# One transposing matmul a pair instead of two, with new instruction orders on every engine

## The chip, the cores and the metric

The kernel runs on one core of a Trainium2 chip. The metric is device time in microseconds (us); of several runs the median counts. One execution was also recorded by the hardware profiler, and all rows below are of that execution.

## The reference

64 samples of 128 channels by 1024 positions pass two residual layers. For sample b:

```
z   = x[b] + w_cond[itok_198[b]]^T @ x[b]              # 128x128 matrix chosen by the sample
out = z + z @ W^T + s * (z @ A^T) @ B^T                # W 1024x1024, adapter of rank 16
A, B, s = lora_A[itok_6[b]], lora_B[itok_6[b]], scalings[itok_6[b]]
```

The adapter has 8 alternatives, the matrix 200. Everything is float32.

## The kernel before

The order of the two layers is exchanged: since the first layer mixes channels and the second mixes positions, the kernel first computes c = x (I + W^T) + adapter and then (I + w_cond)^T c. Samples are taken in 32 pairs. W is cut into 4 by 3 blocks (b00 to b32) of 256 by 342. One pair's big product is a fast matrix multiplication with 19 block products, "17", "5", "15", "13" and so on, in place of 24; their left operands are sums of blocks of x (u, u12, u67, u910, u11, u54, u3 and the plain a001, a02, a03, a1, a13), their right operands sums of W's blocks. Partial results go through six PSUM banks with roles alpha, beta, pi02, pi10, pi11, pi12 that change between even and odd pairs (`BANKS`), and are collected in c10_sb, c11_sb, c12_sb and c02_sb.

For precision each float32 operand is split into a rounded part and a rest (x_hi and x_lo, w_hi and w_lo, z_hi and z_lo, c_hi and c_lo): ScalarE rounds (`copy`), VectorE subtracts, and a product is six TensorE matmuls (two chunks of 128 times three combinations).

The adapter rides along: 16 extra columns on some products give xa = x A^T s, 128 by 16 for each of the two samples. VectorE writes xa and its rest into `xa_cols` (`sum_xa1`, `split_xa1`, `rest_xa1` for sample 1 after product 11; `split_xa0`, `rest_xa0` for sample 0 after product 3). A "turn" is a matmul of xa_cols with an identity that transposes it; ScalarE copies the result to `g_sb` (`turned_xa`), and TensorE multiplies it with `b_stack`, the chosen rows of B, in three `lora` matmuls a sample. Sample 1's are "lora 10, 11, 12", sample 0's "lora 00, 01, 02". Before, turn1 (sample 1, into o_ps) stands behind product 8 and turn0 (sample 0, into the alpha bank) between products 6 and 12, and the three lora matmuls of sample 0 stand behind product 17 of the next pair.

The second layer of pair p is computed during pair p+1: `condition` is three matmuls of 512 columns into o_ps; ScalarE copies o_ps to o_sb (`evacuate`), and SyncE's queue stores it.

The orders are written out by hand: each engine has a program of its own, in which an instruction waits for counters (semaphores) of others and holds up all that stands behind it on its engine. Pairs 0 and 1 are special. Pair 0 is a plain ("dense") product with W's blocks as they land; meanwhile GpSimd adds identities to them (`add_identity`, names i10, i11b, i32 and so on) and VectorE forms the right operands (`add`; the wait `made`). Pair 1 multiplies unsplit float32 operands (`whole_product`) while ScalarE (`in_place`) and VectorE (`split_after`) split the 19 right operands. From pair 2 on all is split; pairs 4 to 29 run in a loop. Adapter rows are split once, saved to DRAM (`save_b`, b_split) and gathered from there for each pair (`load_b`, copied by `take_b`).

## Time and profile before

| | |
|---|---|
| median of 3 runs | 771.11 us (771.02 to 771.27) |
| the profiled execution | 771.08 us, of which the recorded span is 769.2 us |
| TensorE matmuls (PE) | 761.3 us busy, 99% of the span, 4432 instructions |
| VectorE (DVE) | 612.7 us, 80% |
| ScalarE (ACT) | 504.3 us, 66% |
| GpSimd (POOL) | 196.8 us, 26% |
| granted TensorE clock | 1.00 in every slice |
| DMA | 128 GB/s on average, 321 GB/s in the first of 40 slices |

The span runs from the first to the last recorded instruction. Busy time of TensorE is the union of overlapping matmuls: each is recorded from its start to the modelled end of its last column, so the distance between two starts, not the recorded length, is what one matmul costs.

### The profile page before, as it was taken

The numbers are of one execution on the slowest core, as the hardware profiler recorded it, in microseconds if no ns is written. First come the engines' busy times: TensorE is split into PE (matmuls) and PEld (weight loads), VectorE is DVE, ScalarE is ACT, GpSimd is POOL, SyncE is SP. The second block draws the span as 40 slices with busy tenths as digits, with TensorE's granted clock in tenths as the row PEclk, the third lists the DMA queues.
The fourth block names the chain that finished last, engine by engine and source line by source line (L and its number), as shares of the span: only waits on it lengthen the run. The fifth ranks groups of instructions, "written<-read, shape, count | busy, mean of one in ns | idle before, by whom it ended". The sixth has DMA issues, their size and how long they took to land.

```text
span 769.2 us, 16746 instructions
## 1 busy us (share of the span) xinstructions
PE 761.3 (99%) x4432; PEld 721.5 (94%) x4432; DVE 612.7 (80%) x1386; ACT 504.3 (66%) x1173; POOL 196.8 (26%) x428
## 2 busy tenths in 40 slices
PE   8999999999999999999999999999999999999998
PEld 5667999999999999999999999999999999999997
DVE  6899977879777788777888777888777888777774
ACT  3476666676666676666676666676666676666673
POOL 5633211332311333212333211333212233212200
PEclk9999999999999999999999999999999999999999
DMA  9333334442334342334442343442343432343222
GB/s 321 138 131 144 124 121 147 125 149 90 111 128 147 125 148 86 116 127 139 134 144 80 114 140 129 143 132 84 124 137 123 150 129 84 121 143 123 89 90 83
DMA packets 47291, 98.32 MB, mean 128 GB/s; under 512 B 6438, under 2 KB 25894, under 8 KB 47270
## 3 DMA queue, kind: packets, MB, share of 16 engines
q1 hardware_dynamic: 46832, 97.68, 37.6%
q10 hardware_dynamic: 438, 0.39, 0.2%
q8 instruction: 9, 0.15, 0.1%
q14 instruction: 12, 0.10, 0.0%
HBM read 63.45 MB, written 34.60 MB: 127 GB/s over the span
## 4 chain that ended last, share of the span: by engine, by line
PE 90%; DVE 2%; issue 0%; ACT 0%; DVEq 0%; ACTq 0%
PE bank L1394 75%; PE o_ps L1455 4%; PE bank L1433 4%; PE o_ps L1454 4%; PE o_ps L1456 4%; DVE c_sb L904 0%; DVE z_lo L901 0%; DVE x_lo L901 0%; PE o_ps L1445 0%; PE bank L1438 0%; DVE x_raw L901 0%; DVE w_lo L901 0%; ACT z_hi L518 0%; DVE bank L904 0%; PE bank L1454 0%
## 5 line engine op out<-in xcount | busy, mean ns | idle before, releaser
L1394 PE MATMUL bank<-w_hi,x_hi 128*128 128x342 f32 (+2 forms) x1200 | 390.4, 325 | 1.1 <-ACT c_sb L518 1.1
L1394 PE MATMUL bank<-w_lo,x_hi 128*128 128x342 f32 (+2 forms) x1200 | 387.1, 323 | 0.0
L1394 PE MATMUL bank<-w_hi,x_lo 128*128 128x342 f32 (+2 forms) x1200 | 386.5, 322 | 0.0
L1394 PEld LDWEIGHTS bank<-w_hi,x_hi 128*128 128x128 f32 x1200 | 225.8, 188 | 9.7 <-ACT c_sb L518 2.2
L1394 PEld LDWEIGHTS bank<-w_lo,x_hi 128*128 128x128 f32 x1200 | 225.6, 188 | 2.8
L1394 PEld LDWEIGHTS bank<-w_hi,x_lo 128*128 128x128 f32 x1200 | 226.1, 188 | 0.0
L901 DVE TENSOR_TENSOR x_lo<-x_raw,x_hi 128x256 fp32r<-128x256 f32 (+1 forms) x270 | 145.0, 545 | 31.3 <-ACT x_hi L518 26.7
L518 ACT ACTIVATE x_hi<-x_raw 128x256 fp32r<-128x256 f32 (+1 forms) x270 | 133.8, 507 | 53.9 <-PE bank L1394 45.7
L303 POOL TENSOR_TENSOR w_lo<-a_ride,w_hi 128x160 fp32r<-128x160 f32 x30 | 15.6, 521 | 503.5 <-ACT w_hi L518 503.5
L518 ACT ACTIVATE c_sb<-bank 128x342 f32<-128x342 f32 x190 | 85.7, 452 | 41.4 <-PE bank L1394 39.0
L518 ACT ACTIVATE z_hi<-c_sb 128x340 fp32r<-128x340 f32 (+1 forms) x128 | 60.3, 490 | 53.0 <-DVE c_sb L904 53.0
L904 DVE TENSOR_TENSOR c_sb<-bank,c_sb 128x342 f32<-128x342 f32 x186 | 91.1, 504 | 3.6 <-PE bank L1433 2.5
L518 ACT ACTIVATE o_sb<-o_ps 128x512 f32<-128x512 f32 x124 | 73.9, 596 | 12.6 <-PE o_ps L1456 12.6
L901 DVE TENSOR_TENSOR x_lo<-t_sb,x_hi 128x512 fp32r<-128x512 f32 x60 | 41.5, 692 | 36.0 <-ACT x_hi L518 35.9
L901 DVE TENSOR_TENSOR z_lo<-c_sb,z_hi 128x340 fp32r<-128x340 f32 (+1 forms) x128 | 69.6, 545 | 0.4 <-ACT z_hi L518 0.2
L901 DVE TENSOR_TENSOR xa_sum<-bank,c_sb 128x16 f32<-128x16 f32 x31 | 5.4, 174 | 63.1 <-PE bank L1394 63.1
L518 ACT ACTIVATE bank<-bank 128x342 f32<-128x342 f32 (+1 forms) x93 | 41.2, 444 | 16.3 <-PE bank L1394 15.8
L1454 PE MATMUL o_ps<-z_hi,c_hi 128*128 128x512 f32 x126 | 50.5, 401 | 0.0
L1455 PE MATMUL o_ps<-z_lo,c_hi 128*128 128x512 f32 x126 | 49.8, 395 | 0.0
L1456 PE MATMUL o_ps<-z_hi,c_lo 128*128 128x512 f32 x126 | 49.5, 392 | 0.0
L279 POOL TENSOR_TENSOR a_ride<-a_now,s_now 128x32 f32<-128x32 f32 x93 | 43.5, 493 | 17.0 <-DMA a_now<-lora_a 10.2
L1433 PE MATMUL bank<-b_stack,g_sb 128*128 128x340 f32 (+1 forms) x192 | 46.4, 324 | 0.4 <-ACT b_stack L518 0.4
(106 smaller groups left out, 888.1 us busy)
## 6 DMA issues: line engine op xcount, KB each, us to landing
x_raw<-xT SPq DMA_DIRECT2D x62, 512.0 KB, 4.2
out<-o_sb SPq DMA_DIRECT2D x62, 512.0 KB, 2.6
b_stack_raw<-b_split SPq DMA_DIRECT2D x128, 128.0 KB, 2.5
c_raw<-cond_w SPq DMA_DIRECT2D x64, 64.0 KB, 1.7
a_now<-lora_a SPq DMA_DIRECT2D x62, 64.0 KB, 3.2
w_lo_raw<-wB SPq DMA_DIRECT2D x7, 342.0 KB, 8.2
w_hi_raw<-wB SPq DMA_DIRECT2D x5, 342.0 KB, 5.8
out<-x_raw SPq DMA_DIRECT2D x4, 256.0 KB, 2.0
```

The lines of the kernel that those rows point to most:

```text
L279: unit.tensor_tensor(to, a_now[:, n, k:k + count, :], s_now[:, n:n + 1].unsqueeze(2).to_broadcast([P, count, 2 * R]), ALU.mult).then_inc(a ...
L303: unit.tensor_tensor(left_rides(w_lo), rides(0, 5), left_rides(w_hi), ALU.subtract).then_inc(ride_ready, 1)
L518: return nc.scalar.activation(to, x, ACT.Copy)
L901: return nc.vector.tensor_tensor(to, x, y, ALU.subtract)
L904: return nc.vector.tensor_tensor(to, x, y, ALU.add)
L1394: last = nc.tensor.matmul(bank[:, lo:hi], x[:, left, c * C:(c + 1) * C], w[:, c, FIRST[o]:FIRST[o] + WIDTH[o]], start=opens and c == 0 and ...
L1433: nc.tensor.matmul(main_of(bank_of(j, d, role), cols.stop - cols.start), g_sb[n][:, :], b_stack[:, cols], start=False, stop=True, skip_gro ...
L1454: nc.tensor.matmul(bank[:, :], c_hi[:, n, :], z_hi[n][:, cols], start=True, stop=False)
L1455: nc.tensor.matmul(bank[:, :], c_hi[:, n, :], z_lo[n][:, cols], start=False, stop=False)
L1456: nc.tensor.matmul(bank[:, :], c_lo[:, n, :], z_hi[n][:, cols], start=False, stop=True)\
```

## The change

1. Every pair but the last has one turn. Both samples' xa lie in one tile `xa_cols` (rows 0 to 47 and 64 to 111 after the transposition), g_sb of each sample keeps zeros in the other's rows, and ScalarE copies 64 rows for each. The one turn stands between products 19 and 6; the last pair keeps a turn of sample 1 by itself.
2. The end of TensorE's pair is rewritten (`end`): products 1 and 3 before the second `condition`, then 19, the turn, 6, and four lora matmuls (11, 10, 12, 00) before product 12. Two lora matmuls are left behind product 17.
3. ScalarE's and VectorE's pair programs are in another order throughout; pairs 1, 2 and 3 have orders of their own.
4. In the first pair GpSimd reads the adapter numbers before it waits for the table of scalings, and adds b11's identity after the rides of b10 and b00.
5. The two stores of the split adapter rows are issued by ScalarE's queue instead of SyncE's; SyncE gathers pair 0's rows before it loads pair 1's A.

```diff
-             "b11": ("lo", "6"), "b32": ("lo", "16"), "b31": ("lo", "12"), "b02": ("lo", "1"), "b10": ("lo", "3"),
+             "b11": ("lo", "6"), "b32": ("hi", "8"), "b31": ("lo", "12"), "b02": ("lo", "1"), "b10": ("lo", "3"),
...
-    POOL_SUMS = ("i21a", "i21b", "i10", "i11a", "i11b", "i00", "i32", "i22")
+    POOL_SUMS = ("i21a", "i21b", "i10", "i00", "i11a", "i11b", "i32", "i22")
...
-        xa_cols = [sb(f"xa_cols{n}", [P, P], f32) for n in range(2)]
+        xa_cols = sb("xa_cols", [P, P], f32)
...
             def load_b(i, j, d):
                 found = adapters(sp, i, j, d)
-                after(sp, lora_done["00"], i, j, d - 1)
+                after(sp, lora_done["02"], i, j, d - 1)
...
-            sp.wait_ge(b_hi_ready, 1)
-            save_b(0, z_hi[0])
             sp.wait_ge(cond_landed, 16)
             load_c(0, 0, 0)
-            sp.wait_ge(b_lo_ready, 1)
-            save_b(1, z_lo[0])
             sp.wait_ge(adapter_landed, 16)
+            sp.wait_ge(b_saved, 32)
+            load_b(0, 0, 0)
             sp.wait_ge(first_scaled, 8)
             load_a(sp, 0, 0, 1)
-            sp.wait_ge(b_saved, 32)
-            load_b(0, 0, 0)
...
+            first = [pool.value_load(adapter_sb[0:1, n:n + 1], min_val=0, max_val=NAD - 1) for n in range(2)]
             pool.wait_ge(s_tab_ready, 1)
-            pick_scalings(0, 0, 0)
+            for n in range(2):
+                nc.gpsimd.tensor_copy(s_now[:, n:n + 1], s_tab[:, bass.ds(first[n], 1)]).then_inc(s_picked, 1)
...
             add_identity("b10", 0, 256, 0, 86)
-            pool.wait_ge(w_landed["b11"], 16)
-            add_identity("b11", 0, 0, 86, 42)
-            add_identity("b11", 1, 42, 0, 128)
             first_rides("b10")
             pool.wait_ge(w_landed["b00"], 16)
             add_identities("b00", 0)
             first_rides("b00")
+            pool.wait_ge(w_landed["b11"], 16)
+            add_identity("b11", 0, 0, 86, 42)
+            add_identity("b11", 1, 42, 0, 128)
...
             def turned_xa(i, j, d, n):
-                after(act, turned[n], i, j, d)
-                if n:
-                    after(act, lora_done["12"], i, j, d - 1)
+                rows = slice(n * P // 2, (n + 1) * P // 2)
+                alone = n and not exists(i, j, 1)
+                if alone:
+                    act.wait_ge(turned_alone, 1)
                 else:
-                    after(act, lora_done["00"], i, j, d - 1)
-                copy(g_sb[n][:, :], o_ps[1][:, 0:P] if n else bank_of(j, d, "alpha")[:, H - P:H]).then_inc(g_ready[n], 1)
+                    after(act, turned, i, j, d)
+                after(act, lora_done["12" if n else "02"], i, j, d - 1)
+                copy(g_sb[n][rows, :], o_ps[1][rows, 0:P] if alone else bank_of(j, d, "alpha")[rows, H - P:H])\
+                    .then_inc(g_ready[n], 1)
...
+            act.wait_ge(b_hi_ready, 1)
+            save_b(0, z_hi[0])
...
+            act.wait_ge(b_lo_ready, 1)
+            save_b(1, z_lo[0])
...
-            copy_c5(0, 1)
-            hi_z02(0, 1, -1)
-            begin_c10(0, 1)
-            evacuate(0, 1, -1, 1, 0)
+            hi_z02(i, j, -1)
             made(act, "9", "f")
             in_place("9")
-            seed_pi11(0, 1)
-            in_place("8")
-            evacuate(0, 1, -1, 1, 1)
+            evacuate(i, j, -1, 1, 0)
+            begin_c10(i, j)
             made(act, "6", "16")
             in_place("16")
...
+            def end(i, j):
+                left("u3", i, j)
+                multiply("16", "pi12", i, j).then_inc(product_done["16"], 1)
+                after(pe, c02_begun, i, j, 0)
+                left("a001", i, j)
+                multiply("1", "alpha", i, j)
+                multiply("3", "alpha", i, j).then_inc(product_done["3"], 1)
+                if exists(i, j, -1):
+                    condition0(i, j, -1, 1)
+                left("a02", i, j)
+                after(pe, c_block["12"], i, j, -1)
+                multiply("19", "pi02", i, j, True).then_inc(product_done["19"], 1)
+                turn(i, j)
+                after(pe, c02_half, i, j, 0)
+                multiply("6", "beta", i, j).then_inc(product_done["6"], 1)
+                after(pe, g_ready[1], i, j, 0)
+                after(pe, b_ready, i, j, 0)
+                lora("11", i, j, 0)
+                lora("10", i, j, 0)
+                lora("12", i, j, 0)
+                after(pe, g_ready[0], i, j, 0)
+                lora("00", i, j, 0)
+                left("a03", i, j)
+                multiply("12", "beta", i, j).then_inc(product_done["12"], 1)
```

What this does to the order on TensorE at the end of an odd pair of the loop: before, from the first `condition` of sample 0 to the end. Turn1 writes o_ps1, turn0 bank2 (alpha), and xa0_ready and g1_ready are the counters of VectorE's and ScalarE's part of the adapter.

```order
L1456 MATMUL o_ps0<-z_hi0,c_lo 128x512
L1445 MATMUL o_ps1<-ident_r,xa_cols1 128x128 [waits o_out11,xa1_ready]
L1394 MATMUL bank5<-w_hi,x_hi 128x342 [waits u3_ready]
...
L1454 MATMUL o_ps1<-z_hi0,c_hi 128x512 [waits z02_ready,g1_ready]
...
L1394 MATMUL bank2<-w_hi,x_hi 128x358 [waits a001_ready,c02_begun]
...
L1433 MATMUL bank0<-b_stack,g_sb1 128x342 [waits b_ready,g1_ready]
L1433 MATMUL bank1<-b_stack,g_sb1 128x342
...
L1394 MATMUL bank4<-w_hi,x_hi 128x342 [waits c12_summed,a02_ready]
...
L1433 MATMUL bank5<-b_stack,g_sb1 128x340
L1394 MATMUL bank3<-w_hi,x_hi 128x342 [waits c02_half]
...
L1438 MATMUL bank2<-ident_r,xa_cols0 128x128 [waits xa0_ready,a03_ready]
```

And now at the same place:

```order
L1525 MATMUL bank2<-w_hi,x_hi 128x358 [waits a001_ready,c02_begun]
...
L1587 MATMUL o_ps1<-z_hi0,c_hi 128x512 [waits z02_ready,o_out11]
...
L1525 MATMUL bank4<-w_hi,x_hi 128x342 [waits c12_summed,a02_ready]
...
L1571 MATMUL bank2<-ident_r,xa_cols 128x128 [waits xa1_ready,xa0_ready]
L1525 MATMUL bank3<-w_hi,x_hi 128x342 [waits c02_half]
...
L1564 MATMUL bank1<-b_stack,g_sb1 128x342 [waits b_ready,g1_ready]
L1564 MATMUL bank0<-b_stack,g_sb1 128x342
L1564 MATMUL bank5<-b_stack,g_sb1 128x340
L1564 MATMUL bank2<-b_stack,g_sb0 128x342 [waits g0_ready]
L1525 MATMUL bank3<-w_hi,x_hi 128x342 [waits a03_ready]
```

The lora matmuls of both samples now come six matmuls (product 6) behind the one turn, where turn1 had three products and a `condition` between it and its first lora.

ScalarE at the end of an odd pair of the loop, now (before, the two copies to g_sb stood eleven and more instructions apart, each behind its own turn):

```order
L516 ACTIVATE w_hi<-a_ride 128x5x2x16 [waits p3_done,a_summed]
L516 ACTIVATE w_hi<-a_ride 128x4x2x16
L516 ACTIVATE x_hi<-x_raw0 128x256 [waits p19_done,x_landed0_0]
L516 ACTIVATE g_sb1<-bank2 64x128 [waits lora12_done,xa_turned]
L516 ACTIVATE c_hi<-c_raw 128x256 [waits o_done01,ci_summed]
L516 ACTIVATE g_sb0<-bank2 64x128 [waits lora02_done,xa_turned]
L516 ACTIVATE x_hi<-x_raw0 128x512 [waits p6_done,x_landed0_0]
L516 ACTIVATE z_hi0<-bank2 128x342 [waits o_done00,lora00_done]
L516 ACTIVATE o_sb<-o_ps1 128x512 [waits o_done01]
```

What moved: the two g copies stand with one instruction (hi_of_c) between them, behind hi_a02, which waits for product 19.

VectorE between pairs 0 and 1, from the first rest of z on. The rows named w_lo_raw are sums of W's blocks; the one that waits for p17_done is the operand of product 9. Before:

```order
L901 TENSOR_TENSOR z_lo1<-c10_sb,z_hi1 128x342 [waits z10_hi_ready]
L901 TENSOR_TENSOR z_lo1<-c11_sb,z_hi1 128x342 [waits z11_hi_ready]
L1164 TENSOR_TENSOR w_lo_raw<-w_lo_raw 128x2x342 [waits p17_done]
L901 TENSOR_TENSOR z_lo1<-c12_sb,z_hi1 128x340 [waits z12_hi_ready]
L901 TENSOR_TENSOR z_lo0<-bank1,z_hi0 128x342 [waits z01_hi_ready]
L901 TENSOR_TENSOR z_lo0<-bank0,z_hi0 128x342 [waits z00_hi_ready]
```

Now:

```order
L1245 TENSOR_TENSOR w_lo_raw<-w_lo_raw,w_hi_raw 128x2x342 [waits pool_summed]
L964 TENSOR_TENSOR z_lo1<-c10_sb,z_hi1 128x342 [waits z10_hi_ready]
L964 TENSOR_TENSOR z_lo1<-c11_sb,z_hi1 128x342 [waits z11_hi_ready]
L1245 TENSOR_TENSOR w_lo_raw<-w_lo_raw 128x2x342 [waits dve_summed,pool_summed]
L964 TENSOR_TENSOR z_lo0<-bank0,z_hi0 128x342 [waits z00_hi_ready]
L1245 TENSOR_TENSOR w_lo_raw<-w_lo_raw,w_hi_raw 128x2x342 [waits dve_summed,dense_done]
L1245 TENSOR_TENSOR w_lo_raw<-w_lo_raw,w_hi_raw 128x2x342 [waits dve_summed]
L964 TENSOR_TENSOR z_lo1<-c12_sb,z_hi1 128x340 [waits z12_hi_ready]
L964 TENSOR_TENSOR z_lo0<-bank1,z_hi0 128x342 [waits z01_hi_ready]
L1245 TENSOR_TENSOR w_lo_raw<-w_lo_raw,w_hi_raw 128x2x342 [waits p17_done]
```

What moved: z12's rest stands behind four sums (16a, 16, 19a, 19) instead of one, and product 9's sum is the last of all.

## Rows read from the trace of the kernel before

**Rows 1.** The page: busy time of TensorE, and its granted clock in 40 slices.
```profile
PE 761.3 (99%) x4432; PEld 721.5 (94%) x4432; DVE 612.7 (80%) x1386; ACT 504.3 (66%) x1173; POOL 196.8 (26%) x428
...
PEclk9999999999999999999999999999999999999999
```

**Rows 2.** TensorE's waits: waited for, us in total, times, longest.
```profile
PE bank L1566 <- POOL w_hi_raw L465: 1.4, 1, 1.4
...
PE bank L1394 <- ACT c_sb L518: 1.1, 1, 1.1
PE bank L1433 <- ACT b_stack L518: 0.4, 1, 0.4
```

**Rows 3.** TensorE's groups: the two turns (busy us, mean ns).
```profile
L1445 PE MATMUL o_ps<-ident_r,xa_cols 128*128 128x128 f32 x32 | 7.5, 234 | 0.0
L1438 PE MATMUL bank<-ident_r,xa_cols 128*128 128x128 f32 x32 | 7.4, 233 | 0.0
```

**Rows 4.** TensorE in order of time (start, length), around turn1 of a pair.
```profile
406.54 0.32 PE L1394 MATMUL bank<-w_hi,x_lo 128*128 128x342 f32 x1
...
407.39 0.22 PE L1445 MATMUL o_ps<-ident_r,xa_cols 128*128 128x128 f32 x1
407.45 0.37 PE L1394 MATMUL bank<-w_hi,x_hi 128*128 128x342 f32 x1
407.66 0.32 PE L1394 MATMUL bank<-w_lo,x_hi 128*128 128x342 f32 x1
407.82 0.32 PE L1394 MATMUL bank<-w_hi,x_lo 128*128 128x342 f32 x1
```

**Rows 5.** ScalarE in order of time, in the same pair.
```profile
406.90 0.46 ACT L518 ACTIVATE c_sb<-bank 128x342 f32<-128x342 f32 x1 [1.20 <-PE bank L1394]
407.65 0.28 ACT L518 ACTIVATE g_sb<-o_ps 128x128 fp32r<-128x128 f32 x1 [0.30 <-PE o_ps L1445]
407.82 0.60 ACT L518 ACTIVATE o_sb<-o_ps 128x512 f32<-128x512 f32 x1
...
409.84 0.41 ACT L518 ACTIVATE c_hi<-c_raw 128x256 fp32r<-128x256 f32 x1
410.15 0.62 ACT L518 ACTIVATE x_hi<-t_sb 128x512 fp32r<-128x512 f32 x1
```

**Rows 6.** VectorE in order of time, pair 0's sums and first rests of z.
```profile
22.66 0.99 DVE L1164 TENSOR_TENSOR w_lo_raw<-w_hi_raw,w_lo_raw 128x684 f32<-128x684 f32 x1 [0.81 <-POOL w_lo_raw L472]
23.58 0.41 DVE L904 TENSOR_TENSOR x_whole<-x_raw 128x256 f32<-128x256 f32 x1
...
33.79 2.65 DVE L1164 TENSOR_TENSOR w_lo_raw<-w_lo_raw,w_hi_raw 128x684 f32<-128x684 f32 x3
36.36 0.93 DVE L901 TENSOR_TENSOR z_lo<-c_sb,z_hi 128x342 fp32r<-128x342 f32 x2
```

**Rows 7.** ScalarE in order of time, pair 1.
```profile
42.29 0.60 ACT L518 ACTIVATE o_sb<-o_ps 128x512 f32<-128x512 f32 x1 [0.23 <-PE o_ps L1456]
42.78 0.77 ACT L518 ACTIVATE w_hi<-w_lo_raw 128x684 fp32r<-128x684 f32 x1
```

**Rows 8.** TensorE in order of time, pair 1: the second condition, product 2.
```profile
42.98 0.65 PE L1454 MATMUL o_ps<-z_hi,c_hi 128*128 128x512 f32 x1
...
43.94 1.36 PE L1410 MATMUL bank<-w_lo_raw,x_whole 128*128 128x358 f32 x4
```

**Rows 9.** DMA: the second load of pair 1's x, issue and time to landing.
```profile
L336 SPq DMA_DIRECT2D x_raw<-xT x1: 1096/1096/1096, 12.2 to 12.2; - x1
...
DMA to landing us min/median/max: 10.0/10.0/10.0
```

**Rows 10.** DMA: all queues together, 14 to 21 us.
```profile
DMA packets 1602, 2.70 MB, mean 386 GB/s; under 512 B 109, under 2 KB 1360, under 8 KB 1602
```

**Rows 11.** TensorE in order of time, product 2 of pair 2.
```profile
72.11 0.43 PE L1394 MATMUL bank<-w_hi,x_hi 128*128 128x358 f32 x1 [1.06 <-ACT c_sb L518]
72.38 0.33 PE L1394 MATMUL bank<-w_lo,x_hi 128*128 128x358 f32 x1
```

More of the change, by code:

```diff
@@ new lines, in step, with last_step @@
+                hi_u11(i, j, 1)
+                hi_rides(i, j, 1)
+                hi_a02(i, j, 1)
+                turned_xa(i, j, 0, 1)
+                hi_of_c(i, j)
+                turned_xa(i, j, 0, 0)
+                hi_a001(i, j, 1)
+                hi_z00(i, j, 0)
+                evacuate(i, j, -1, 0, 1)
+                hi_z11(i, j, 0)
+                hi_z10(i, j, 0)
+            def last_step(i, j):
+                copy_c17(i, j)
+                hi_a03(i, j, 0)
+                hi_z12(i, j, -1)
+                copy_c5(i, j)
+                hi_z01(i, j, -1)
+                begin_c10(i, j)
+                evacuate(i, j, -1, 1, 0)
+                seed_pi11(i, j)
+                hi_z02(i, j, -1)
+                begin_c11(i, j)
+                hi_u54(i, j, 0)
+                evacuate(i, j, -1, 1, 1)
+                seed_pi10(i, j)
+                take_b(i, j)
+                begin_c12(i, j)
+                seed_pi12(i, j)
@@ new lines, in step @@
+                sum_u3(i, j, 1)
+                rest_u(i, j, 1)
+                rest_u12(i, j, 1)
+                rest_a13(i, j, 1)
+                sum_xa1(i, j)
+                split_xa1(i, j)
+                rest_a1(i, j, 1)
+                clear_beta(i, j)
+                sum_v(i, j, 1)
+                rest_xa1(i, j)
+                sum_u67(i, j, 1)
+                half_c02(i, j)
+                sum_u910(i, j, 1)
+                rest_u67(i, j, 1)
+                sum_u11(i, j, 1)
@@ new lines, in _ @@
+            clear_beta(i, j)
+            rest_a13(i, j, 1)
+            sum_xa1(i, j)
+            rest_a1(i, j, 1)
+            split_xa1(i, j)
+            sum_v(i, j, 1)
+            sum_u3(i, j, 1)
+            sum_u67(i, j, 1)
+            half_c02(i, j)
+            rest_xa1(i, j)
+            split_xa0(i, j)
+            sum_u910(i, j, 1)
+            rest_xa0(i, j)
+            add_identity_c(i, j)
+            sum_u11(i, j, 1)
+            half_c12(i, j)
+            rest_u910(i, j, 1)
@@ L1574, in _ @@
             for _ in range(7):
[L1575 removed]
+                nc.tensor.matmul(o_ps[1][:, 0:P], xa_cols[:, :], xa_cols[:, :], start=True, stop=True)
             dense("b12")
@@ L1598, in _ @@
             pe.wait_ge(ident_r_ready, 1)
-            turn1(0, 0)
-            turn0(0, 0)
+            turn(0, 0)
             made(pe, "i32")
             dense("b32")
+            pe.wait_ge(zeros_ready, 3)
             after(pe, g_ready[1], 0, 0, 0)
@@ L1607, in _ @@
             lora("12", 0, 0, 0)
+            after(pe, g_ready[0], 0, 0, 0)
+            lora("00", 0, 0, 0)
             made(pe, "i22")
```

528 lines of the change are left out of this document (294 added, 234 removed).

## The prediction

> **What bounds the kernel now.** I read the page first. TensorE is busy for 99% of the span and its clock is granted in full in every slice [rows 1], so the end can only move if TensorE gets less to do, or if the few places where it stands still change. Next the list of its waits [rows 2]: 1.4 us for GpSimd's identity in b21, 1.1 us for ScalarE's copy of c10_sb in pair 2, 0.4 us for the adapter rows b_stack in pair 0. The first and the last lie in the first 35 us. There is no wait in pairs 3 to 31. So in the steady part a matmul that goes away is worth exactly what it costs, provided that the new orders of ScalarE and VectorE bring nothing late; in the first three pairs the question is who is late.
>
> **What a turn costs.** There are 32 of each kind, recorded at 0.23 us [rows 3], but that is not the price. In order of time turn1 starts at 407.39, the next product at 407.45 and that product's second matmul at 407.66; ordinary neighbours start 0.16 apart [rows 4]. From the turn to the second matmul it is 0.27, so the turn costs 0.27 - 0.16 = 0.11 us: 0.06 of its own and 0.05 since the following weights could not be loaded behind so short a matmul. The Trainium skill, "TensorE: Matmul & The Clock Gate", section "Back-to-back issue gap", gives some 81 ns for a sustained matmul of 128 columns; by it the 31 turns would be worth 2.5 us as an estimate, while the trace has more, and the trace is taken.
>
> All pairs but the last lose one turn: 31 x 0.11 = 3.4 us. The lora matmuls, products and conditions are the same in number and width, so moving them costs TensorE nothing by itself. The three lora matmuls of sample 0 that stood behind product 17 become two there and one in the group of four.
>
> **Is the new turn in time, and what waits for it?** I lay a pair out around the turn's start, T. Latencies are from the trace: from the start of a product's last matmul to the dependent ScalarE copy 0.36 (406.54 to 406.90); from a turn's start to the copy of g 0.26 (407.39 to 407.65); that copy lasts 0.28 and lets the next start after 0.17; a 256-column copy such as hi_of_c holds ScalarE for 0.31 (409.84 to 410.15) [rows 4, 5]. Product 19's last matmul starts at T-0.16, so hi_a02 starts at T+0.20, the copy of g1 at T+0.51 (end T+0.79), hi_of_c at T+0.68, the copy of g0 at T+0.99 (end T+1.27). TensorE does product 6 in 0.06 + 0.21 + 5 x 0.16 = 1.07 and wants lora 11 at T+1.07, whose weights g1 it wants one matmul earlier, at T+0.91; lora 00 comes three matmuls later, with g0 wanted at T+1.39. Both copies are in time, each by 0.12 us. That is the thinnest margin of the change. On the other side of the turn, xa of sample 0 needs product 3, then VectorE: between product 3 and the turn now lie the second condition and product 19, about 1.6 us, against two small VectorE operations and one 512-column rest between them; an estimate of 0.4 us is left. The other waits that moved (evacuation of o_ps1 now at the very end of a pair, sample 0's z00 rounded before the pair ends, SyncE's store and load of c behind that evacuation) have half a microsecond or more before their reader. I cost them at nothing; they are covered by product 12 and the next pair's product 17.
>
> **The first pair.** GpSimd's earlier read and the later b11 take away most of the 1.4 us, and the rows of B, saved by ScalarE's queue, come before the lora matmuls: up to 1.4 + 0.4 = 1.8 us of lead for TensorE at the start of pair 1 [rows 2]. I do not think that it keeps it. VectorE works without a pause from 23.58 on, through the three sums that end at 36.4, to the rests of z [rows 6]; it is the engine that the start of pair 1 depends on, and what it still has to do grows. Behind those three sums the new order has sum 16a, z10, z11, sum 16, z00, sums 19a and 19, z12, z01, and sum 9. A sum costs 2.65 / 3 = 0.87, a rest of z 0.43 (a pair of them in 0.93, and the next starts sooner) [rows 6]. z12 is thus ready at 36.4 + 4 x 0.87 + 4 x 0.43 = 41.6, sum 9 at 36.4 + 5 x 0.87 + 5 x 0.43 = 42.9. The second condition of pair 1, which stood at 42.98 [rows 8], would want z12 at about 41.2 with the full lead; a first small wait. Then ScalarE: it now does in_place("9"), which waits for the last of VectorE's sums, then the evacuation, and only then begin_c10, for which product 2 waits. The rounding of a whole block holds it for some 0.66, the evacuation for 0.49 (42.29 to 42.78), the copy lasts 0.46 [rows 5, 7]: product 2 cannot start before 42.9 + 0.66 + 0.49 + 0.46 + 0.1 = 44.6. It stood at 43.94 [rows 8].
>
> To this comes a delay D of VectorE's whole row of sums. Below, D is 0, or rather a little less than nothing if the sums find their blocks sooner. Above: VectorE began on pair 1's x at 23.58, the second half of which had landed at 12.2 + 10.0 = 22.2 [rows 6, 9]; the two stores of 0.5 MB each used to stand behind these loads in SyncE's queue and now go beside them. At 386 GB/s over all queues [rows 10] 1 MB is 2.7 us, so x lands up to 24.9 and D is at most 1.3. The Trainium skill says in "DMA: Bandwidth & Descriptors", section "Queues, rings and completion order", that each DMA engine takes turns between the rings of its queues; by that rule the loads would indeed give way to the stores, which speaks for the upper half. No run here shows two such queues side by side yet. I take D = 0.6, between the ends, since the stores need not overlap with all the loads: VectorE has also to wait for GpSimd's b32, once 0.81 us [rows 6], which is now later by b11. Product 2 starts at 45.2, which is 1.3 later than before, with the front's lead gone.
>
> **Pair 2.** Here TensorE stood 1.06 us and restarted at half pace (72.11 to 72.38, 0.27 for 0.16), 1.2 us together [rows 2, 11], because hi_u54, which waited for VectorE, stood ahead of begin_c10 on ScalarE. The new order has begin_c10 ahead of it, and VectorE has left rests out of pair 1's tail. I count the 1.2 us as won.
>
> **The sum.** -3.4 (turns) + 1.3 (product 2 in pair 1) - 1.2 (pair 2) = -3.3; a few tenths more come from having fewer short groups of lora matmuls among the float32 products of pair 1, which I put at 0.2. The profiled execution took 771.08, the median is 771.11, so it is the same base: 771.1 - 3.5 = **767.6 us**.
>
> **The rivals.**
> - *The front's lead is kept.* Sums and z12 come in time (VectorE is faster than its rows, or D is negative), product 2 is not held, and the 1.8 us of waits are won as well. 771.1 - 3.4 - 1.8 - 1.2 - 0.2 = 764.5. For it: all three named waits are dealt with by the change. Against: the ScalarE and VectorE rows as added up above. Chance 0.22.
> - *The loads give way fully, and pair 2 stays late.* D = 1.3 adds 0.7, and VectorE's seven or so splits in pair 2 keep a wait like the old one (1.2): 769.5. Chance 0.13.
> - *The saved turn is paid back in waits.* Both g copies have 0.12 us to spare. If they come 0.1 late, every steady pair (29 of them) loses what it saved: 767.6 + 29 x 0.11 = 770.8, no change. Chance 0.11.
> - *Slower: the second g copy decides.* ScalarE is a single file: hi_rides, hi_a02, g1, hi_of_c, g0. If anything ahead of hi_a02 is 0.4 us late (hi_u11, which hangs on VectorE's sum_u11 and through it on hi_u67), g0 is late by 0.28; with the 0.11 of an interrupted weight load [rows 11] it is 0.39 a pair, and 29 x 0.39 = 11.3 gives 778.9. It becomes a loss when the copies are later than their margin by more than about 0.12, that is, when ScalarE reaches hi_a02 later than T+0.44. Between no change and this I take 773 as its time. Chance 0.07.
> - *The forecast*, 766.8 to 768.5: chance 0.47.
>
> **How the numbers follow.** Faster by over 0.2% (1.5 us, about what a measurement can tell from no change; below 769.6) are the forecast, the first rival and nearly all of the second: 0.81. Within 0.2%: the third and the rest of the second, 0.12. Slower: 0.07. The range holds the forecast, the first two rivals and leaves out the last two: 764.4 to 769.6.
>
> **What would show it.** One turn a pair, and the distance between the same matmul of two neighbouring pairs shorter by 0.11 than in the old trace, with TensorE's list of waits empty after pair 3: the steady term is right. In the list of waits the 1.4 us for GpSimd's identity much smaller, and in its place one for ScalarE's c10_sb (product 2 of pair 1, at about 45) and perhaps VectorE's z_lo just before: the front's term is right. Waits of TensorE for g_sb in every pair would mean the third or fourth rival; product 2 of pair 1 before 43 the first. The prediction is wrong if VectorE gets through its sums at another pace than in the old trace, or if a wait appears in the middle of the steady pair where I found half a microsecond of room.

## The result, and the profile of the changed kernel

The change made the kernel slower.

| | before | changed |
|---|---|---|
| median (runs) | 771.19 us (4 runs, 771.02 to 771.45) | 780.04 us (4 runs, 779.06 to 782.82) |
| ratio, 95% interval | | 1.012 (1.0093 to 1.0148) |
| profiled execution, its span | 771.08 us, 769.2 us | 779.06 us, 777.3 us |

The forecast was 767.6. One sees first what was gained as foretold. TensorE has 31 matmuls fewer than in [rows 1], its clock is granted in full in the profiled execution, and it is still "busy" for 99% of the span. The page:

```profile
PE 766.7 (99%) x4401; PEld 718.8 (92%) x4401; DVE 616.9 (79%) x1387; ACT 516.8 (66%) x1173; POOL 174.0 (22%) x428
...
PEclk9999999999999999999999999999999999999999
```

TensorE's waits, to be set against [rows 2] (waited for, us in total, times, longest):

```profile
PE bank L1541 <- issue: 2.6, 1, 2.6
PE bank L1564 <- ACT b_stack L516: 1.9, 1, 1.9
...
PE bank L1722 <- POOL w_hi_raw L460: 0.9, 1, 0.9
PE bank L1587 <- DVE z_lo L964: 0.3, 1, 0.3
```

And those of its weight loads (PEld):

```profile
PEld bank L1564 <- ACT g_sb L516: 8.0, 28, 0.3
PEld bank L1541 <- issue: 2.8, 1, 2.8
```

The wait of 1.1 us for c_sb in pair 2 is gone. The list of the matmuls' own waits shows no other repeated wait, and whoever stops there sees waits that are 2.2 us longer in all (6.9 against 4.7) for a loss of 8. The line that matters is in the list of weight loads: 28 times 0.3 us for g_sb. The fourth lora matmul follows three others without a gap of its own in the record, so its late weights do not count as idle time of the matmuls.

The chain shows the same by distances. Product 2 of a pair opens a piece of 60 matmuls; starts (and lengths) of those of pairs 2, 3, 4 and 31, the changed kernel and then the one before:

```profile
73.89 9.68 PE bank L1525 x60
97.34 9.68 PE bank L1525 x60
120.40 9.68 PE bank L1525 x60
...
752.49 9.68 PE bank L1525 x60
```

```profile
72.11 10.16 PE bank L1394 x60
96.02 9.70 PE bank L1394 x60
119.20 9.70 PE bank L1394 x60
...
744.65 9.68 PE bank L1394 x60
```

From pair 4 to pair 31 the 27 pairs take 632.09 / 27 = 23.41 us each against 23.17. With these starts the loss of the profiled execution adds up:

| stretch | changed minus before |
|---|---|
| to product 2 of pair 1 (47.22 against 43.94 in [rows 8]) | +3.3 |
| from there to product 2 of pair 2 (26.67 against 28.17) | -1.5 |
| to product 2 of pair 3 (23.45 against 23.91) | -0.5 |
| to product 2 of pair 4 (23.06 against 23.18) | -0.1 |
| 27 pairs of 23.41 against 23.17 | +6.6 |
| behind product 2 of pair 31 (24.8 against 24.55) | +0.3 |
| span | +8.1 |

The other runs bring one more term. The four had a mean granted clock of 1.000 (779.06 us), 1.000 (779.33), 0.998 (780.75) and 0.996 (782.82), while the kernel before has 0.999 or 1.000 in all its runs, these four within half a microsecond; the median is thus about 1 us above the profiled execution. e3 below shows what such a fall of the clock looks like; the changed kernel's own two longest runs have no trace, so that it is the same there is inferred from their mean clock.

**The steady pair.** ScalarE around a turn that starts at 416.11, to be set against [rows 5]:

```profile
416.37 0.42 ACT L516 ACTIVATE x_hi<-x_raw 128x256 fp32r<-128x256 f32 x1 [1.08 <-PE bank L1525]
416.81 0.27 ACT L516 ACTIVATE g_sb<-bank 64x128 fp32r<-64x128 f32 x1
417.11 0.42 ACT L516 ACTIVATE c_hi<-c_raw 128x256 fp32r<-128x256 f32 x1
417.55 0.27 ACT L516 ACTIVATE g_sb<-bank 64x128 fp32r<-64x128 f32 x1
417.72 0.62 ACT L516 ACTIVATE x_hi<-x_raw 128x512 fp32r<-128x512 f32 x1
```

TensorE in the same stretch, to be set against [rows 4]:

```profile
416.11 0.22 PE L1571 MATMUL bank<-ident_r,xa_cols 128*128 128x128 f32 x1
416.17 0.37 PE L1525 MATMUL bank<-w_hi,x_hi 128*128 128x342 f32 x1
416.37 0.32 PE L1525 MATMUL bank<-w_lo,x_hi 128*128 128x342 f32 x1
...
417.15 1.14 PE L1564 MATMUL bank<-b_stack,g_sb 128*128 128x342 f32 x4
418.13 0.32 PE L1525 MATMUL bank<-w_hi,x_hi 128*128 128x342 f32 x1
```

And the weight loads of the four lora matmuls:

```profile
417.13 0.46 PEld L1564 LDWEIGHTS bank<-b_stack,g_sb 128*128 128x128 f32 x3
417.87 0.19 PEld L1564 LDWEIGHTS bank<-b_stack,g_sb 128*128 128x128 f32 x1 [0.28 <-ACT g_sb L516]
```

Four lora matmuls take 0.98 from their start to the next product instead of 4 x 0.16 = 0.63. Look at the distances on ScalarE: hi_a02 to g1 0.44, g1 to hi_of_c 0.30, hi_of_c to g0 0.44. Each is the length of the copy ahead plus 0.02 or 0.03. None of these three copies starts before the one ahead of it has ended, where the forecast let each start 0.1 earlier.

**The start.** TensorE in pairs 0 and 1; the last line is product 2, which stood at 43.94 [rows 8]:

```profile
30.31 0.48 PE L1571 MATMUL bank<-ident_r,xa_cols 128*128 128x128 f32 x1
...
35.06 0.86 PE L1564 MATMUL bank<-b_stack,g_sb 128*128 128x342 f32 x4 [1.92 <-ACT b_stack L516]
...
38.95 0.74 PE L1564 MATMUL bank<-b_stack,g_sb 128*128 128x342 f32 x2
42.25 2.59 PE L1541 MATMUL bank<-w_lo_raw,x_whole 128*128 128x358 f32 x8 [2.57 <-issue]
...
46.27 0.65 PE L1587 MATMUL o_ps<-z_hi,c_hi 128*128 128x512 f32 x1
...
47.22 1.06 PE L1541 MATMUL bank<-w_lo_raw,x_whole 128*128 128x358 f32 x3
```

The profile names no releaser for the 2.57 us ahead of product 5. Other engines do. SyncE's wait for the store of B's rests, in its list of waits:

```profile
SPq L402 <- DMA b_split<-z_lo: 11.5, 1, 11.5
```

SyncE's queue in order of time, the gather of B and the load of pair 1's A:

```profile
28.78 1.78 SPq L346 DMA_DIRECT2D b_stack_raw<-b_split  x4
31.87 1.09 SPq L329 DMA_DIRECT2D a_now<-lora_a  x2
```

GpSimd, from that A to the last ride columns of product 5:

```profile
34.44 2.12 POOL L281 TENSOR_TENSOR a_ride<-a_now,s_now 128x32 f32<-128x32 f32 x3 [10.80 <-DMA a_now<-lora_a]
...
41.58 0.57 POOL L508 COPY w_lo_raw<-a_ride 128x128 f32<-128x128 f32 x1
```

SyncE waits 11.5 us for the store of the rests of B, issues the gather, and only then pair 1's A, at 31.87 (23.86 before). GpSimd has that A at 34.4 and writes the ride columns of product 5 until 42.15; product 5 starts 0.1 later.

VectorE shows a second effect of the stores' new queue. It now stands for pair 1's x, which the kernel before took up at 23.58 without a wait [rows 6]:

```profile
24.34 0.43 DVE L967 TENSOR_TENSOR x_whole<-x_raw 128x256 f32<-128x256 f32 x1 [0.86 <-DMA x_raw<-xT]
```

All five traced kernels that store on ScalarE's queue have this wait (0.86 here and, of the experiments below, 0.92 in e2, 1.72 in e11, 1.74 in e3, 1.85 in e1). The nine that store on SyncE's queue do not have it.

### The profile page after: what moved, and what is told of

Read it like the earlier page. It is cut to its first block, busy times and chain, and to the rows that moved or that the text cites. A ratio compares the mean times of both kernels' runs of the same rounds, so it can differ in the third digit from the quotient of the medians.

```text
span 777.3 us, 16671 instructions
## 1 busy us (share of the span) xinstructions
PE 766.7 (99%) x4401; PEld 718.8 (92%) x4401; DVE 616.9 (79%) x1387; ACT 516.8 (66%) x1173; POOL 174.0 (22%) x428
## 4 chain that ended last, share of the span: by engine, by line
PE 94%; DMA 3%; SPq 1%; issue 1%; ACT 0%; DVE 0%; ACTq 0%; DVEq 0%
PE bank L1525 74%; PE bank L1564 5%; PE o_ps L1588 4%; PE o_ps L1589 4%; PE o_ps L1587 4%; PE bank L1541 3%; DMA b_split<-z_lo 1%; DMA b_raw<-lora_b 1%; SPq L319 0%; DMA b_stack_raw<-b_split 0%; PE bank L1722 0%; ACT z_hi L516 0%; SPq L313 0%; PE bank L1571 0%; ACTq L766 0%
## 5 line engine op out<-in xcount | busy, mean ns | idle before, releaser
L964 DVE TENSOR_TENSOR x_lo<-x_raw,x_hi 128x256 fp32r<-128x256 f32 (+1 forms) x270 | 152.6, 573 | 51.1 <-ACT x_hi L516 51.0
L967 DVE TENSOR_TENSOR c_sb<-bank,c_sb 128x342 f32<-128x342 f32 x186 | 88.7, 502 | 3.7 <-PE bank L1564 2.5
L964 DVE TENSOR_TENSOR z_lo<-c_sb,z_hi 128x340 fp32r<-128x340 f32 (+1 forms) x128 | 65.8, 532 | 2.8 <-ACT z_hi L516 2.6
L516 ACT ACTIVATE z_hi<-c_sb 128x340 fp32r<-128x340 f32 (+1 forms) x128 | 58.7, 486 | 2.5 <-DVE c_sb L967 2.4
L1564 PE MATMUL bank<-b_stack,g_sb 128*128 128x342 f32 (+1 forms) x192 | 50.4, 347 | 2.1 <-ACT b_stack L516 1.9
L1564 PEld LDWEIGHTS bank<-b_stack,g_sb 128*128 128x128 f32 x192 | 31.8, 188 | 13.3 <-ACT g_sb L516 8.0
```

Of the source, the lines that this page charges most:

```text
L516: return nc.scalar.activation(to, x, ACT.Copy)
L964: return nc.vector.tensor_tensor(to, x, y, ALU.subtract)
L967: return nc.vector.tensor_tensor(to, x, y, ALU.add)
L1564: nc.tensor.matmul(main_of(bank_of(j, d, role), cols.stop - cols.start), g_sb[n][:, :], b_stack[:, cols], start=False, stop=True, skip_gro ...
```

## The experiments

The kernel before ran on the same chip beside each of them: 771.2 us (medians of 13 to 27 runs, 770.9 to 771.24, each within about 1.5 us).

### Two tests of the g copies

e1 changes the loop's order on ScalarE and nothing else:

```diff
                 hi_rides(i, j, 1)
-                hi_a02(i, j, 1)
                 turned_xa(i, j, 0, 1)
-                hi_of_c(i, j)
                 turned_xa(i, j, 0, 0)
+                hi_of_c(i, j)
+                hi_a02(i, j, 1)
                 hi_a001(i, j, 1)
```

> The changed kernel with one edit: in ScalarE's pair program (loop and pair 30) both copies of g stand directly behind hi_rides, then hi_of_c, then hi_a02. Theory A (the second g copy, held behind hi_a02 and hi_of_c, is 0.28 us late for lora 00 in each of 28 pairs, which with the slow restart costs 0.34 a pair): the period falls from 23.39 to 23.06, TensorE's weight loads wait no longer for g_sb, and the time is 780 - 28 x 0.34 = 770.5. Rival B (something else stretches the pair, the g wait is only where it shows): less than 2 us gained, a wait appears at another place of the pair.

Measured: 773.31 us (10 runs, 770.52 to 774.38), ratio to before 1.0021 (1.001 to 1.0031); 6.7 less than the changed kernel. The weight loads no longer wait for g_sb, and the pairs are 23.11 apart (122.93 to 746.86 in 27). That is theory A. The fastest runs of the two kernels are 8.5 us apart, near 28 pairs of 0.30; the median gained less, since nine of the ten runs have a mean clock of 0.998 or less.

e2 leaves the order of the changed kernel and copies all 128 rows for each g (the rows meant to be zero then hold the other sample's part, so the adapter's contribution is not the reference's). The two memsets that zeroed those rows at the start, and TensorE's wait for them, are left out as well:

```diff
-                rows = slice(n * P // 2, (n + 1) * P // 2)
+                rows = slice(0, P)
```

> The changed kernel, order untouched, but each copy of g takes all 128 rows instead of 64, and the rows that should be zero carry the other sample's part: the adapter's contribution is wrong, the work of TensorE is the same. Theory A1 (a copy on 64 rows does not overlap with the copy before it, so that it starts 0.44 behind hi_a02 instead of 0.31): the spacing goes back to 0.31 and 0.17, the second copy comes 0.27 us sooner and the wait all but goes, time about 771. Rival A2 (the spacing has to do with the counters that these copies wait for, not with the rows): the spacing stays 0.44, 0.30, 0.44 and the time stays at 780.

Measured: 772.38 us (10 runs, 770.46 to 775.01), ratio 1.0015 (1.0003 to 1.0028), pairs 23.10 apart. ScalarE in e2, turn at 412.55:

```profile
412.81 0.42 ACT L516 ACTIVATE x_hi<-x_raw 128x256 fp32r<-128x256 f32 x1 [1.08 <-PE bank L1523]
413.13 0.26 ACT L516 ACTIVATE g_sb<-bank 128x128 fp32r<-128x128 f32 x1
413.29 0.41 ACT L516 ACTIVATE c_hi<-c_raw 128x256 fp32r<-128x256 f32 x1
413.60 0.27 ACT L516 ACTIVATE g_sb<-bank 128x128 fp32r<-128x128 f32 x1
```

Same order, same lengths, and the distances are 0.32, 0.16 and 0.31, as the forecast had them. More work in the copy makes g0 0.4 us sooner. So it is the 64-row form of the copies that costs, 0.12 to 0.14 at each of three places. The same counters are waited for in both, which speaks against rival A2.

### Two tests of the start

e3 loads A before B on SyncE's queue, as before the change, and leaves the stores on ScalarE's queue:

```diff
-            sp.wait_ge(b_saved, 32)
-            load_b(0, 0, 0)
             sp.wait_ge(first_scaled, 8)
             load_a(sp, 0, 0, 1)
+            sp.wait_ge(b_saved, 32)
+            load_b(0, 0, 0)
```

> The changed kernel, but SyncE loads pair 1's A ahead of gathering pair 0's rows of B, as before; the stores stay in ScalarE's queue. Theory (A of pair 1, now issued behind the gather at 31.9, makes GpSimd's rides late and product 5 of pair 1 stand 2.6 us): the 2.57 wait goes; product 2 of pair 1 is then held by begin_c10 at about 45 instead of 47.2, so 2 us are gained, time about 778. Rival: VectorE is bound all the way to pair 2 and the wait only moves there; under 0.7 us gained.

Measured: 778.67 us (4 runs, 777.7 to 780.4), ratio 1.0094 (1.0076 to 1.0113), 1.4 less than the changed kernel where 2 were expected. The pause before product 5 is gone, and another takes its place, 1.87 us for ScalarE's c10_sb ahead of product 2, which starts at 45.58. TensorE there and behind, and below it the granted clock (stretch, us, PE busy, clock, DMA share, GB/s):

```profile
45.58 4.42 PE L1541 MATMUL bank<-w_lo_raw,x_whole 128*128 128x358 f32 x8 [1.87 <-ACT c_sb L516]
```

```profile
44.00:45.00 1.00, 0.00 (x0) 1.00 0.00 0
45.00:46.00 1.00, 0.42 (x1) 0.90 0.78 246
46.00:47.00 1.00, 1.00 (x3) 0.50 0.89 229
47.00:48.00 1.00, 1.00 (x3) 0.50 0.19 57
48.00:49.00 1.00, 1.00 (x3) 0.50 0.00 0
49.00:50.00 1.00, 1.00 (x4) 0.89 0.00 0
```

Product 2 takes 4.42 us instead of 2.62: after the pause the clock stood at its lower level for some 3.4 us, and the pause of 1.9 cost 3.7 us. e1's profiled execution has the same behind its pause of 4.09 us before product 5: a clock of 0.50 from 44 to 47 us, and 4.28 us for product 5 instead of 2.6.

e4 undoes the whole of part 5 of the change: A first as in e3, and the stores back on SyncE's queue.

```diff
-            act.wait_ge(b_hi_ready, 1)
-            save_b(0, z_hi[0])
...
-            act.wait_ge(b_lo_ready, 1)
-            save_b(1, z_lo[0])
...
+            sp.wait_ge(b_hi_ready, 1)
+            save_b(0, z_hi[0])
             sp.wait_ge(cond_landed, 16)
             load_c(0, 0, 0)
+            sp.wait_ge(b_lo_ready, 1)
+            save_b(1, z_lo[0])
```

> The changed kernel with its part 5 undone: both stores of the split rows and SyncE's order as before. If the stores beside the loads cost VectorE time (x of pair 1 landed 0.8 later), this is better than the run that only restores the order of the two loads, by up to 0.8 us: 777.5. If the queue of the stores does not matter (they end at 27.4 in both traces), the two are equal within 0.3 us.

Measured: 777.66 us (4 runs, 776.99 to 779.0), ratio 1.0084 (1.0067 to 1.0101). A is issued at 21.5, product 5 has no wait, product 2 of pair 1 starts at 43.87 and that of pair 2 at 71.39, 0.7 sooner than before the change. The longest pause behind 30 us is 0.8. The loop is as slow as in the changed kernel (23.41). Against e3 the medians differ by 1.0, but the four runs of each overlap, and those at a clock of 1.0 are equal (777.51 and 777.82 here, 777.70 and 777.75 in e3); so the time does not tell which expectation holds. The traces show what the queue does in the profiled executions: in e3 VectorE waited 1.74 us for x and began on it at 24.86, here it began at 23.17 without a wait, and product 2 of pair 1 starts 1.7 sooner here.

### Both repairs, and their parts

e5 is e1's diff and e4's together.

> The changed kernel with both repairs: in the loop ScalarE copies g1 and g0 before hi_of_c and hi_a02, and the two stores of B's split rows and the load of A before B are on SyncE's queue as they were in the kernel before. Theory: the loss has three parts, the late g0 in every steady pair (0.30 us a pair between the loops of e4_part5_undone and e1_g_copies_first, 23.41 against 23.11), the late ride of product 5, and a drop of the granted clock that sometimes follows that pause. In e4_part5_undone product 2 of pair 2 stood at 71.39 and that of pair 4 at 118.60; 28 pairs at 23.11 instead of 23.41 give 777.7 - 8.4 = 769.3 us, 2 us faster than before, with no weight load waiting for g_sb, no pause over 1 us from 35 us on, a granted clock of 1.0 in nearly all runs and a scatter of about 1 us like that of before. Rival: the scatter of 4 us and the clock of 0.995 to 0.999 belong to the denser loop with one turn; then the median is near 771.5 and the clock stays under 1 in most runs.

Measured: 769.83 us (11 runs, 769.17 to 770.38), ratio 0.9982 (0.9973 to 0.9991), clocks of 0.999 and 1.000. Faster than both kernels, as the theory has it; the denser loop does not bring the clock down, so the rival falls. Pairs are 23.105 apart (119.39 to 743.22 in 27).

e8 is e5 with e3's diff taken back: B before A, the stores still on SyncE's queue.

> As e5_copies_first_stores_back, but SyncE loads B before the A of pair 1, as the changed kernel does; the stores stay on SyncE's queue. Theory: it is this order that makes product 5 late, since SyncE waits for the store to land before it issues A: A at about 31.9 instead of 21.5, TensorE stands 2.5 to 4.1 us before product 5 of pair 1, the granted clock falls to 0.50 for some 3.5 us behind it in most runs, and the median is 772 to 774 with clocks of 0.995 to 0.999. Rival: the store on ScalarE's queue makes it late; then this kernel takes the time of e5_copies_first_stores_back.

Measured: 772.34 us (10 runs, 770.53 to 772.76), ratio 1.0009 (1.0 to 1.0019). Its runs fall in two groups: three at a clock of 1.0 take 770.53 to 770.69, seven at 0.997 or 0.998 take 771.86 to 772.76. The profiled one is of the first group and stands 2.13 us before product 5. The pause itself costs 0.8 over e5's time, and the second group another 1.8. That this is a fall of the clock as in e3 is inferred from the mean clocks, since no run of the second group has a trace.

e11 is the fourth corner, e1's diff and e3's: stores on ScalarE's queue, A before B.

> The changed kernel with g1 and g0 copied first and A of pair 1 loaded before B, the stores of the split rows still on ScalarE's queue: the fourth corner beside e1 (stores on ScalarE's queue, B first: 773.3), e8 (SyncE's, B first: 772.3) and e5 (SyncE's, A first: 769.8). If order and queue add up, 773.3 - 2.5 = 770.8, the queue being worth 1.0. Rival: beside A first the queue is what makes product 2 of pair 1 wait for c10_sb (1.87 us in e3, at 45.58), with a clock of 0.50 behind it in most runs: 771.5 to 772.5, as bad as e8.

Measured: 769.69 us (10 runs, 769.22 to 772.17), ratio 0.9985 (0.9976 to 0.9994). Both expected medians (770.8, and 771.5 to 772.5) were too high: the median is e5's. The rival's wait is there in the profiled execution, but the lower clock in three runs of ten and not in most. Six runs at a clock of 1.0 lie between 769.22 and 769.72 and one at 770.68, three at 0.998 between 771.26 and 772.17; the profiled one is of these, with a pause of 1.88 us for c10_sb and product 2 taking 4.11. With both orders known, the order on SyncE's queue is worth 3.6 us (e1 against e11) or 2.5 (e8 against e5), while the queue that carries the stores is worth 1.0 with B first (e1 against e8) and nothing in the median with A first, though in the profiled execution of e11 x came 1.72 us late for VectorE and product 2 started at 45.76 where e5 has 44.10.

e7 puts hi_of_c alone behind g0, on top of e4.

```diff
                 hi_a02(i, j, 1)
                 turned_xa(i, j, 0, 1)
-                hi_of_c(i, j)
                 turned_xa(i, j, 0, 0)
+                hi_of_c(i, j)
```

> The changed kernel with the stores and the load order of before and one swap in the loop: hi_of_c behind the copy of g0, hi_a02 still ahead of both copies. Theory (a copy of 64 rows starts only when the copy ahead of it has ended): with T the start of the turn, hi_a02 at T+0.26, g1 at T+0.70, g0 at T+1.00 with its end at T+1.27, and g0 is wanted at T+1.39: no wait for g0. g1 ends at T+0.97 where T+0.91 to 1.02 is wanted, so at most 0.1 us a pair is left. The distance of pairs is 23.11 to 23.2, the median 769.3 to 771.5. Rival: hi_a02 ahead of the copies is what makes them late; then 0.2 or more a pair stays and the median is above 774.

Measured: 770.26 us (10 runs, 769.54 to 770.91), ratio 0.9987 (0.9978 to 0.9996), pairs 23.13 apart. The copy of g0 starts 0.30 behind that of g1 and is in time, as the theory has it; what is left is 0.03 a pair. One instruction between the two copies decided 0.28 us a pair.

e12 is e4 with the changed kernel's order, g1 copied on 128 rows and g0 on 64.

> e4_part5_undone with the order of the changed kernel in the loop (hi_rides, hi_a02, g1, hi_of_c, g0), but g1 copied on all 128 rows and g0 on its 64; the rows of g1 that should be zero then hold the other sample's part, so the adapter part of sample 1 is not what it should be. It tells what it is in a 64-row copy that costs. Theory 1, any 64-row copy waits for the end of the copy ahead: g1 0.31 behind hi_a02, hi_of_c 0.16 behind g1, g0 0.44 behind hi_of_c, so at T+1.17 with its end at T+1.44, 0.05 late: the distance of pairs is 23.13 to 23.17, the median 770.0 to 771. Theory 2, it is the change to another first row (g1 begins at row 64, so its own start and the next copy's both wait) and a copy of rows 0 to 63 overlaps like any other: g0 0.31 behind hi_of_c, at T+1.04, no wait, 23.10, median 769.3 to 769.8. The rows of ScalarE decide, not the time.

Measured: 769.91 us (10 runs, 768.89 to 770.38), ratio 0.9984 (0.9975 to 0.9994), pairs 23.11 apart. ScalarE, turn at 412.22:

```profile
412.48 0.42 ACT L523 ACTIVATE x_hi<-x_raw 128x256 fp32r<-128x256 f32 x1 [1.08 <-PE bank L1525]
412.80 0.26 ACT L523 ACTIVATE g_sb<-bank 128x128 fp32r<-128x128 f32 x1
412.96 0.41 ACT L523 ACTIVATE c_hi<-c_raw 128x256 fp32r<-128x256 f32 x1
413.26 0.26 ACT L523 ACTIVATE g_sb<-bank 64x128 fp32r<-64x128 f32 x1
```

A copy of rows 0 to 63 starts 0.30 behind hi_of_c, like one of 128 rows. That is theory 2: with g1 no longer a copy that begins at row 64, none of its neighbours is held apart. It does not explain all of it: in the changed kernel g0, rows 0 to 63, also waited for the end of hi_of_c (0.44), with g1 one instruction further ahead. The hold between hi_a02 and g1, with no other 64-row copy near, speaks for the first row as the cause; but no run has g1 on rows 64 to 127 with g0 on 128 rows, so that is not settled.

### The store of B's rows

e6 changes the scratch tensor from [adapter, part, row, position] to [part, adapter, row, position], so that a store writes 128 equal rows one behind the other; a gather then takes its two parts from two places. It stands on e5.

```diff
-b_split = nc.dram_tensor("b_split", [NAD, 2, R, T]
+b_split = nc.dram_tensor("b_split", [2, NAD, R, T]
...
-b_split[bass.ds(found[n], 1), :, :, :].rearrange("a s r o -> (a s r) o"))
+b_split[:, bass.ds(found[n], 1), :, :].rearrange("s a r o -> s (a r) o"))
```

> As e5_copies_first_stores_back, and the scratch tensor for B's split rows is laid out by part first, so that each store writes 128 rows that follow each other instead of 8 blocks with a gap. Theory: the store lands late because its outer dimension is 8, so that few engines carry it; then it lands before 25 us instead of 27.4, the gather is issued some 2 to 3 us sooner than 28.4, the wait for b_stack (0.8) goes, and product 2 of pair 1 is held by c10_sb instead, so that 0.2 to 0.8 us are won: 768.5 to 769.1. Rival: the store is late because it is queued behind the weights and x on all engines; then it lands at 27.4 as before and nothing changes.

Measured: 1056.75 us (4 runs, 1053.86 to 1058.15), ratio 1.3708 (1.3687 to 1.3729). The store was not the story. It did land sooner, the first gather being issued at 26.25 instead of 28.7. But the gathers, 128 KB each and four of them one behind the other in every pair, now landed after 7.0 to 8.4 us in the first two pairs; in the other kernels that gather 32 rows at once the median is 2.5. Waits of e6 over all engines:

```profile
ACT b_stack L523 <- DMA b_stack_raw<-b_split: 299.5, 32, 10.7
...
PE bank L1526 <- ACT c_sb L523: 203.8, 30, 7.7
```

With pauses of that length in every pair TensorE's granted clock is 0.878 on average. The Trainium skill says in "DMA: Bandwidth & Descriptors", section "Why a DMA increments its semaphore by 16 and not by 1", that the number of engines for a transfer is the largest up to 16 that divides the slowest dimension of both sides. By that rule 2 engines carried e6's gathers and 8 the stores of the changed kernel. The traces agree: from 32 to 38 us, where e6 moves hardly anything but these gathers, the busy share of its 16 DMA engines is 0.13 (2 of 16), and in the changed kernel it is 0.50 to 0.53 (8 of 16) from 23 to 26 us, when the store of B's rests was still under way. e10 makes the dimension 16.

e10 keeps e6's layout and makes the gather of eight transfers of 16 rows, on top of e9 below.

```diff
-                        sp.dma_start(b_stack_raw[row:row + 2 * R, :],
-                                     b_split[bass.ds(found[n], 1), :, :, :].rearrange("a s r o -> (a s r) o"))\
+                      for part in range(2):
+                        sp.dma_start(b_stack_raw[row + part * R:row + (part + 1) * R, :],
+                                     b_split[part, bass.ds(found[n], 1), :, :].rearrange("a r o -> (a r) o"))\
```

> As e9_take_b_later with the scratch tensor laid out by part, and the gather in eight transfers of 16 rows instead of four with an outer dimension of 2. Theory: the number of the outermost dimension sets how many engines carry a transfer (8 for the stores of before, 2 for the gather of e6_store_layout, which took 7 to 8 us for 128 KB instead of 2.5). With 128 rows for the stores and 16 for the gathers both are quick: the store of z_lo lands near 25, b_stack is copied some 1 us sooner than at 33, the 1.2 us that TensorE stands for it in pair 0 falls under 0.4, and the median is 768.2 to 768.9. Rival: eight issues a pair hold SyncE's queue for 1.4 us more (0.35 each), x or the stores of out come late in the steady pairs, and the time is 770 or more.

Measured: 770.02 us (11 runs, 769.09 to 771.35), ratio 0.9985 (0.9976 to 0.9993). The theory is right in what the gathers do, and its 768.2 to 768.9 is wrong; the rival has the time. The gathers (64 KB each now) land after 2.1 us, the wait for b_stack falls to 0.2 us and the loras start at 33.70 (35.35 in e9). Then product 2 of pair 1 waits 0.89 for c10_sb and starts at 44.11 all the same, and later pairs are dearer: some are 23.2 or 23.3 long instead of 23.1, and the 27 from pair 4 on take 1.9 us more than e9's. What comes late there is the gather itself and not x or a store: ScalarE waits for it 30 times, 40.3 us in all, against 10 times and 6.7 in e9. That the eight issues a pair cause it was not tested by itself.

e9 is e5 with take_b in pair 1 moved behind seed_pi10. In e5 TensorE stood 0.96 us before product 10, because ScalarE waited 1.42 us for a gather with the seed behind it.

```diff
             hi_u12(i, j, 1)
-            take_b(i, j)
             hi_u(i, j, 1)
             evacuate(i, j, -1, 1, 1)
             seed_pi10(i, j)
+            take_b(i, j)
```

> e5_copies_first_stores_back, and in pair 1 ScalarE takes b_stack of that pair behind seed_pi10 instead of ahead of hi_u. In e5 ScalarE stood 1.42 us for the gather at 48.94 and seeded pi10 only at 50.68, and TensorE stood 0.96 us before product 10 at 51.19. Theory: the wait for the gather holds the seed; with it behind, product 10 starts at about 50.2 and the 0.96 us and the second of slower starts are won: 769.8 - 0.9 = 768.9, granted clock 1.0. Rival: the seed was late for the evacuation ahead of it or product 10 waits for another operand; then the time stays at 769.8.

Measured: 768.36 us (7 runs, 767.75 to 770.88), ratio to before 0.9966 (0.9955 to 0.9978). Product 10 has no wait (50.63 after a product that started at 49.48). This is the best version, 0.5 under the 768.9 of the theory, 2.9 us under the kernel before and 11.7 under the changed one. The one run at 770.88 has a clock of 0.998.

## Why the prediction was wrong

**The step that failed** is "Both copies are in time, each by 0.12 us". The latencies in front of it were nearly right: hi_a02 started at T+0.26 and not T+0.20, and g0 was wanted where the forecast had it: in e2, where nothing is late, its weights load at T+1.38 (forecast T+1.39). What was wrong is "that copy lasts 0.28 and lets the next start after 0.17" [rows 5]. That row is a copy of 128 rows; the change copies 64, and the form was never in the old trace. Three distances of 0.17 or 0.31 became 0.30 or 0.44, in sum with the 0.06 it is 0.45, so g0 ended at T+1.71 where T+1.39 was wanted. 0.32 late agrees with the loop: 23.41 against 23.11 with the copies in time (e1, e2, e5, e9, e11, e12). The Trainium skill, "ScalarE: Activation LUTs", section "What ACT_TABLE_LOAD costs", has back-to-back ACTIVATEs overlap by some 93 ns; the 128-row copies here agree (0.42 long, 0.32 apart), those around g1 do not.

**The fourth rival** named the place and worked out nearly the price (0.39 a pair and 778.9, against 0.30 and 780.0), though it then took 773 as its time, between no change and that; and it named another cause: something ahead of hi_a02 late by 0.4 us. Nothing was. It got 0.07, since a margin of 0.12 us in 29 pairs was taken for a margin. A thin margin in a repeated place should have held much more of the chance.

**The turn's price** of 0.11 us was right in pair 3, whose ScalarE order copies g before hi_a02 (23.06 against 23.18). In the loop only 0.06 was left, 23.105 against 23.165, also where no copy was late. In e1's chain the 12 matmuls behind the lora group take 1.93 us in a loop pair and 1.89 in pair 3; which wait this is was not tested. The term of 3.4 us was worth about 1.8.

**The first pair.** "The rows of B, saved by ScalarE's queue, come before the lora matmuls" was wrong. The gather could be issued at 28.7 in both kernels, though the second store was issued at 16.5 instead of 18.7, and the wait for b_stack grew from 0.4 [rows 2] to 1.9: the turn came 0.9 sooner and the copy of b_stack 0.5 later (33.86 against 33.37). GpSimd's wait fell from 1.4 only to 0.9, and is 0.8 to 1.6 in the variants: in e4, where GpSimd was ready first, it stood for the landing of b21 itself until 10.24. The limit from VectorE and ScalarE was named rightly, but its two terms were off in opposite ways. Without the stores beside the loads (D = 0) product 9's sum ended at 42.18 and product 2 started at 43.87 (e4), where the forecast had 42.9 and "cannot start before" 44.6. And D was larger than the 0.6 taken: the sum ended 1.0 later in the changed kernel (43.20), and VectorE's wait for x was 1.7 in e3 and e11, beyond the 1.3 that the forecast allowed. So that product 2 stood for c10_sb until 45.58 (e3) and 45.76 (e11), forecast 45.2, is near by luck. What was not seen at all is that SyncE now waited for that store with the load of pair 1's A behind it. The diff shows both lines, and the prediction followed B's rows and never asked what A's load fed. It cost 2.0 us more than the forecast's 1.3 (+3.3), and on other runs the clock.

**Pair 2** was right: 1.5 us between the two product 2, forecast 1.2 and 0.2.

**The clock** had no term. The forecast priced waits at their length, where e3's pause of 1.87 us cost 3.7.

## What to carry to other kernels

- Where a copy or a matmul changes its form (rows, first row, width), the old trace's spacing is not a measurement of it. If the margin is thinner than the unmeasured step, and the place repeats in every iteration, give the miss most of the chance, and read the weight loads' waits as well as the matmuls'.
- When a wait is moved ahead of a DMA on a queue, follow that DMA to its last reader. Here two swapped lines on SyncE's queue were worth 2.5 to 3.6 us; and with TensorE at 99% a pause of 1.9 us cost 3.7 (e3), since the clock fell behind it.

## What the runs showed of the hardware

- A ScalarE copy of 64 rows that begins at row 64 starts 0.02 us after the end of the copy ahead, and the next starts after its end as well (0.44 and 0.30 from start to start), while with 128 rows, or with rows 0 to 63 and g1 on 128 rows (e12), it starts 0.1 before that end. Why g0 waited too in the changed kernel stays open.
- TensorE's granted clock fell from its upper level (1.00) to its lower (0.50) for about 3.4 us after pauses of 1.88 (e11), 1.87 (e3) and 4.09 us (e1), and did not after 2.57 (the changed kernel), 2.55 (e2) and 2.13 (e8). The length of the pause alone thus does not tell. With e8 it differs from run to run: seven of ten were 1.3 to 2.2 us longer at a mean clock of 0.997 or 0.998.
- A gather of 128 KB, the four of a pair issued one behind the other, took 2.5 us (median) with an outermost dimension of 32 rows and 7.0 to 8.4 with one of 2, while 0.13 of the 16 DMA engines was busy (e6).
- Two stores of 512 KB issued on ScalarE's queue while SyncE's queue loaded x made VectorE wait 0.86 to 1.85 us for x in five traces; on SyncE's queue behind those loads they made it wait in none.
